# Pairing the score products of the first cross attention on two 64-row tiles of TensorE

## The reference, cut to what matters

```python
def _L0_xattn_ref(query, key_value, mask, Wq, bq, Wk, bk, Wv, bv, Wo, bo):
    E = 128; H = 16; D = E // H            # 16 heads of 8 features
    Q = (query @ Wq.T + bq).reshape(B, Lq, H, D)
    K = (key_value @ Wk.T + bk).reshape(B, Lkv, H, D)
    V = (key_value @ Wv.T + bv).reshape(B, Lkv, H, D)
    scores = jnp.einsum('bqhd,bkhd->bhqk', Q, K) / jnp.sqrt(jnp.float32(D))
    scores = jnp.where(mask[:, None, None, :] == 0, -jnp.inf, scores)
    probs = jax.nn.softmax(scores, axis=-1)
    context = jnp.einsum('bhqk,bkhd->bqhd', probs, V).reshape(B, Lq, E)
    return context @ Wo.T + bo
...
x = x + _L0_xattn_ref(_layernorm(x, axis=-1), ctx_1024, mask_BxS2_ik0, ...)
```

## Time and profile before

| | us |
|---|---|
| Runs of the kernel before | 1927.71, 1927.79, 1922.93 (median 1927.71) |
| Profiled execution | 1924.5, its span 1922.8 |
| TensorE matmul busy in the span | 1362.7 (71%) |
| VectorE busy | 1442.3 (75%) |
| ScalarE busy | 1132.0 (59%) |
| GpSimd busy | 1141.2 (59%) |
| First cross attention, first score to last addition | 205.3 to 437.4 |
| Score products of `x0` on TensorE (L856), busy | 137.7 |
| Masked keys on ScalarE (L994), 128 instructions | 63.0 |

### The profile page before, as it was taken

How to read it: one execution, slowest core, us unless ns; L and a number is a source line. 1 busy time by engine, 2 the same in 40 slices (tenths; PEclk the granted TensorE clock), 3 DMA queues, 4 the chain that set the end, 5 groups by cost and what they waited for, 6 DMA issues and landing times. The chain is left out here.

```text
span 1922.8 us, 23528 instructions
## 1 busy us (share of the span) xinstructions
PE 1362.7 (71%) x6930; PEld 713.1 (37%) x6931; DVE 1442.3 (75%) x2463; ACT 1132.0 (59%) x2507; POOL 1141.2 (59%) x742
## 2 busy tenths in 40 slices
PE   3778899995655566665565656655545899999968
PEld 2555677772311112221112212211102566666522
DVE  3554588885509999999999999999993577666734
ACT  2443888875636556555555665555533777677720
POOL 2001455660029999999999999999980344333400
PEclk8898899997667777877787777777767899999979
DMA  3000000000044324343333333233303000000000
GB/s 104 1 2 2 1 2 1 1 2 1 0 144 188 127 95 154 130 158 154 154 155 118 127 133 151 114 153 154 155 1 88 1 1 1 1 0 1 1 0 22
DMA packets 51978, 134.49 MB, mean 70 GB/s; under 512 B 19076, under 2 KB 28568, under 8 KB 39448
## 3 DMA queue, kind: packets, MB, share of 16 engines
q1 hardware_dynamic: 49112, 130.78, 18.0%
q10 hardware_dynamic: 2496, 2.36, 0.4%
q0 software_dynamic: 256, 0.01, 0.0%
HBM read 114.26 MB, written 18.87 MB: 69 GB/s over the span
## 5 line engine op out<-in xcount | busy, mean ns | idle before, releaser
L1493 POOL TENSOR_TENSOR ma_hs<-ma_dtuR,ma_Bt 128x1024 f32<-128x1024 f32 x256 | 596.9, 2359 | 20.3 <-PE ps L1569 13.5
L1652 ACT ACTIVATE ps<-ma_dtR,ma_A 128x512 f32<-128x512 f32 x512 | 332.6, 682 | 345.2 <-DVE ma_hs L1786 286.7
L809 POOL TENSOR_TENSOR x_pr<-x_pr,x_rec 128x512 f32<-128x512 f32 x256 | 268.0, 1047 | 355.5 <-DVE x_rec L1058 355.5
L1780 DVE TENSOR_TENSOR_SCAN ps<-ps,ma_hs 128x1024 f32<-128x1024 f32 x176 | 401.6, 2282 | 0.0
L1569 PE MATMUL ps<-ma_hs,ma_fold 128*32 128x512 f32 x1024 | 178.9, 834 | 207.7 <-POOL ma_hs L1501 175.7
L1024 ACT ACTIVATE x_pr<-x_sm,x_mx 128x256 f32<-128x256 f32 x512 | 254.6, 500 | 56.1 <-DVE x_mx L1049 55.2
L1786 DVE TENSOR_TENSOR ma_hs<-ps,ma_Ct 128x1024 f32<-128x1024 f32 x176 | 215.4, 1224 | 6.1
L1536 PE MATMUL ps<-ma_hn,ma_w_tap 128*128 128x512 f32 (+3 forms) x256 | 145.4, 722 | 95.7 <-ACT ma_hn L1670 84.0
L1780 DVE TENSOR_TENSOR_SCAN ma_hs<-ps,ma_hs 128x1024 f32<-128x1024 f32 x80 | 182.5, 2281 | 33.4 <-ACT ps L1652 33.4
L1501 POOL TENSOR_TENSOR ma_hs<-ma_hs,ma_Ct 128x1024 f32<-128x1024 f32 x80 | 188.3, 2354 | 22.9 <-DVE ma_hs L1780 22.9
L880 PE MATMUL ps<-ident,x_pr 128*128 128x128 f32 x1024 | 158.8, 279 | 0.8 <-DVE x_pT L955 0.4
(11 more groups left out here) (307 smaller groups left out, 2245.2 us busy)
## 6 DMA issues: line engine op xcount, KB each, us to landing
ma_dtuR<-ma_dtu_d SPq DMA_DIRECT2D x32, 1024.0 KB, 8.0
ma_dtR<-ma_dt_d SPq DMA_DIRECT2D x32, 1024.0 KB, 9.9
ma_Bt<-ma_bc_d SPq DMA_DIRECT2D x16, 1024.0 KB, 4.9
ma_Ct<-ma_bc_d SPq DMA_DIRECT2D x16, 1024.0 KB, 6.8
ma_dtu_d<-ma_dtu SPq DMA_DIRECT2D x32, 256.0 KB, 2.0
ma_dt_d<-ma_dt SPq DMA_DIRECT2D x32, 256.0 KB, 2.3
ma_cwb<-in_L_attn_conv_w_dram SPq DMA_DIRECT2D x4, 512.0 KB
x_m<-in_mask_BxSxS_fk_dram SPq DMA_DIRECT2D x1, 2048.0 KB, 11.2
```

What stands on the lines that cost most here:

```text
L809: pool.tensor_tensor(pr[:, r, :, :], pr[:, r, :, :], rec[:, r, :].unsqueeze(2).broadcast_to([P, 2, L]), ALU.mult).then_inc(pr_done, 1)
L1493: pool.tensor_tensor(hs[:, k % SLOTS, :, :], dtuR[:, unit(f, h), q, :].unsqueeze(1).broadcast_to([P, 2, CH]), rows(Bt, k), ALU.mult).then_ ...
L1652: e = act.activation(c.ps[:, 2 * (k % 2) + a, :], dtR[:, unit(f, h), q, :], ACT.Exp, scale=A[:, (f // QUARTERS) % 2, h, q, no:no + 1])
L1780: dve.tensor_tensor_scan(out, pair(k), slot(k), 0.0, ALU.mult, ALU.add).then_inc(scan_done, 1)
```

## The change

It touches `x0` alone. The recurrent stage of layer 1 (with eleven C products on VectorE) and every other stage are the same in both kernels.

1. `head` maps steps n and n+1 (n even) to two heads a and a+8, whose features lie in rows 0 to 63 and rows 64 to 127.
2. `mine` has two columns per a, for a and a+8; a new reduction on VectorE adds them into `member`. One masked copy of the keys (`keys_of_pair`) then serves both heads, and `km` has 8 entries in place of 16.
3. `score` goes; `x0` uses `score_pair`, in even steps, with the keys from `km`. Four PSUM banks hold scores: 0, 1 and 5, 7 in turn. The wait is that the maximum of head n-3 has been taken.
4. The projections use bank 6 alone, and each waits for the evacuation of the one before it. The three units move to steps 9, 10 and 11.
5. `out_projection` writes bank 6 too. It waits for the last evacuation of the projections, and unit 0 of the next ones waits for `finish`.
6. In `weigh` the four heads of a group take the column tiles in the order 0, 2, 1, 3 in place of 0, 1, 2, 3.

```diff
-    WO = 5 if small else 7
+    WO = 6 if small else 7
+    SCORE_BANKS = ((0, 1), (5, 7)) if small else ((0, 1),)
...
-        return 4 * (n % 4) + n // 4 if small else n
+        return n // 4 + 4 * (n // 2 % 2) + 8 * (n % 2) if small else n
...
         def units(n):

             a = n - FIRST_UNIT
+            if small:
+                return range(a - 1, a) if 1 <= a <= NP else range(0)
             return range(min(NP, a * 3 // 2), min(NP, (a + 1) * 3 // 2)) if a >= 0 else range(0)
...
+        def score_bank(n):
+
+            return SCORE_BANKS[(n // 2) % len(SCORE_BANKS)][n % 2]
+
+        def projection_bank(n):
+
+            return 6 if small else 6 + n % 2
...
                 def project(b, n, first, second):

-                    bank = c.ps[:, 6 + n % 2, :]
-                    if n >= 2:
+                    bank = c.ps[:, projection_bank(n), :]
+                    if small and n >= 1:
+                        pe.wait_ge(evac, b * NP + n)
+                    elif n >= 2:
                         pe.wait_ge(evac, b * NP + n - 1)
                     elif not first:
                         pe.wait_ge(evac, b * NP)
...
-                    if n >= 2 or not first:
+                    if small and (n >= 4 or not first):
+                        pe.wait_ge(max_done, b * NH + n - 2)
+                    elif not small and (n >= 2 or not first):
                         pe.wait_ge(s_free, b * NH + n)
+                    if small:
+                        pe.wait_ge(km_done, b * (NH // 2) + n // 2 + 1)
                     for t in range(2):
                         for r in range(2):
                             row = slice(64 * r, 64 * r + 64)
-                            mm = pe.matmul(c.ps[:, r, t * L:(t + 1) * L], q[row, p, n // 2, t * P:(t + 1) * P],
-                                           k[row, p, n // 2, :], start=True, stop=True)
+                            queries = q[row, p, 0 if small else n // 2, t * P:(t + 1) * P]
+                            keys = km[row, p, n // 2, :] if small else k[row, p, n // 2, :]
+                            mm = pe.matmul(c.ps[:, score_bank(n + r), t * L:(t + 1) * L], queries, keys, start=True, stop=True)
                             if t == 1:
                                 mm.then_inc(scores, 1)
...
-                    if not small and not last:
+                    if not last:
                         pe.wait_ge(evac, b * NP + NP)
...
-                def keys_of_head(b, p, n):
-
-                    h = head(n)
-                    act.activation(km[:, p, h, :], k[:, p, :], ACT.Copy, scale=mine[:, h:h + 1]).then_inc(km_done, 1)
+                def keys_of_pair(b, p, n):
+
+                    a = head(n)
+                    act.activation(km[:, p, n // 2, :], k[:, p, :], ACT.Copy, scale=member[:, a:a + 1]).then_inc(km_done, 1)
...
                 if small:
                     dve.wait_ge(consts, 4)
+                    dve.tensor_reduce(member[:, :], mine[:, :, :], AX.X, ALU.add).then_inc(member_done, 1)
```

More of the change, by code:

```diff
@@ L747, in cross_attention_stage @@
             mr = s.sb("mr", [P, 2, L])
-            km = s.sb("km", [P, 2, NH, L])
-            mine = s.sb("mine", [P, NH])
+            km = s.sb("km", [P, 2, NH // 2, L])
+            mine = s.sb("mine", [P, NH // 2, 2])
+            member = s.sb("member", [P, NH // 2])
         (consts, ctx_in, proj, evac, neg_done, km_done, scores, s_free, shifted, max_done,
-         exp_done, rec_done, pr_done, turned, pT_done, pv, oT_done, out_done, x_done) = (s.sem(n) for n in (
+         exp_done, rec_done, pr_done, turned, pT_done, pv, oT_done, out_done, x_done, member_done) = (s.sem(n) for n in (
             "consts ctx_in proj evac neg_done km_done scores s_free shifted max_done exp_done "
-            "rec_done pr_done turned pT_done pv oT_done out_done x_done").split())
+            "rec_done pr_done turned pT_done pv oT_done out_done x_done member_done").split())
         flat = pr[:, :, :, :].rearrange("p a t k -> p (a t k)")
@@ L794, in _ @@
                     pool.memset(v[:, :, :, :], 0.0).then_inc(consts, 1)
[L795 removed]
+                    pool.memset(mine[:, :, :], 1.0).then_inc(consts, 1)
                     pool.wait_ge(consts, 2)
[L798 to L799 removed]
+                    pool.affine_select(out=mine[:, :, :], in_=mine[:, :, :], compare_op=ALU.is_ge, fill=0.0, base=0,
+                                       pattern=[[-D, NH // 2], [-64, 2]], channel_multiplier=1).then_inc(consts, 1)
                     pool.wait_ge(consts, 3)
[L801 to L802 removed]
+                    pool.affine_select(out=mine[:, :, :], in_=mine[:, :, :], compare_op=ALU.is_ge, fill=0.0, base=D - 1,
+                                       pattern=[[D, NH // 2], [64, 2]], channel_multiplier=-1).then_inc(consts, 1)
                 def body(b, p, fresh, first, last):
@@ L845, in project @@
                     mm.then_inc(proj, 1)
[L847 to L850, removed]
-                    if n >= 2 or not first:
-                        pe.wait_ge(max_done, b * NH + n - 1)
-                    h = head(n)
[L854 to L858, removed]
                 def score_pair(b, p, n, first):
@@ L931, in body @@
                     for n in range(NH):
-                        if small:
-                            score(b, p, n, first)
-                        elif n % 2 == 0:
+                        if n % 2 == 0:
                             score_pair(b, p, n, first)
@@ L999, in _ @@
                     act.wait_ge(evac, NQK)
-                    for n in range(4):
-                        keys_of_head(0, 0, n)
+                    act.wait_ge(member_done, 1)
+                    for n in range(0, 4, 2):
+                        keys_of_pair(0, 0, n)
                 def step(b, p, n, first):
@@ L1012, in body @@
                                 evacuate(b + 1, 1 - p, a, False, first)
-                        if small and n + 4 < NH:
-                            keys_of_head(b, p, n + 4)
-                        elif small and not last:
+                        if small and n % 2 == 0 and n + 4 < NH:
+                            keys_of_pair(b, p, n + 4)
+                        elif small and n % 2 == 0 and not last:
                             if n + 4 == NH:
                                 act.wait_ge(evac, b * NP + NP + NQK)
-                            keys_of_head(b + 1, 1 - p, n + 4 - NH)
+                            keys_of_pair(b + 1, 1 - p, n + 4 - NH)
                         step(b, p, n, first)
@@ L1040, in maximum @@
                     dve.wait_ge(scores, b * NH + n + 1)
-                    bank = c.ps[:, n % 2, :].rearrange("p (t k) -> p t k", t=2)
+                    bank = c.ps[:, score_bank(n), :].rearrange("p (t k) -> p t k", t=2)
                     if n >= 2 or not first:
```

2 lines of the change are left out of this document (removed).

## The result

The change makes the kernel faster by about half of what was forecast. Median 1914.69 us in four runs (1913.99 to 1914.89), against 1925.33 us (1922.93 to 1927.79, four runs) for the kernel before: ratio 0.9944, 95% interval 0.993 to 0.9957, so -10.6 us (-8 to -13.5) where -22.9 was forecast (from 1924.5; between the medians, 1927.7 to 1903, it was -24.7). The profiled execution has 1914.0 us (span 1912.2) against 1924.5 (span 1922.8).

The account below looks back on a forecast made before the run. TensorE was taken to bound `x0`, busy 165.89 of 169.90 us. Six periods falling from 28.3 to 25.2 us save 18.6; with 4.3 + 2.5 - 2.5 at the edges, 22.9: 1924.5 to 1901.6, median 1903, range 1885 to 1919.

Parts of the forecast that it names:

- The loop of 5.67 us through `weigh`: In `x0`, the chain from VectorE's copy through `weigh`, turn and pair to the next group's copy: 5.67 us for four heads.
- the limit of 3: Sign of a wrong forecast in `x0`: the wait before the projection units exceeds 3 us a period.
- the edges: `x0` outside the six middle periods: 4.3 us saved before, 2.5 behind, 2.5 lost at the start.
- the waits add up: Rival in `x0`: extra waits at `weigh` or projections give a 27.0 us period, 1917 us, gain 11; chance 0.18.
- Together 1.8 us a period: Projections of `x0` in one bank: VectorE loses 1.15 and 0.95 us, 0.27 of it already counted; 1.8 us a period.
- the layout from the end of maximum 8: Times through the projections of `x0`: unit 0 at 1.35 us, pair 10 at 2.31, unit 2 at 5.0.
- The 0.58 that the forecast added for `output_bank` and `finish`: In a period of `x0` these two add 0.85 us, of which 0.27 falls into the loop's wait.
- 169.90 / 6 = 28.3: Period of one batch element in `x0` before the change, from seven `output_bank` instructions: 28.3 us.
- The rest of the kernel should only be shifted: Everything from 437 us on, behind `x0`, was to be only shifted in time.
- VectorE's bound: Rival in `x0`: TensorE gets ahead, VectorE sets a 22.5 us period; 1885 us, gain 43, chance 0.16.
- The 0.05 put on the clock: Chance of 0.05 given to the clock; a clock below 0.95 in `x0` would show the forecast wrong.
- The pair without overlap: Rival in `x0`: the two row tiles do not overlap, period 31.1 us, slower by 22; chance 0.01.

Follow-up runs that it names:

- Whole rows: Kernel after with each score product over all 128 rows instead of 64, so a pair cannot share the array: 1934.14 us, ratio 1.0057 to the kernel before.
- two banks: Kernel after with score pairs on two score banks, projections and output bank as before the change: 1951.08 us, ratio 1.0121 to the kernel before.
- finish first, loop written out: Kernel after with `finish` ahead of maximum 8, unit 2 one step later and no hardware loop in `x0`: 1899.28 us, ratio 0.9866.
- Finish first: Kernel after with `finish` ahead of maximum 8 on VectorE and unit 2 one step later, in step 12: 1907.27 us, ratio 0.99.
- The loop written out: Kernel after with the eight batch elements of `x0` written one after another, without the hardware loop: 1909.7 us, ratio 0.9923.
- the shift: Five idle products (2.2 us) ahead of the last output projection of `x1`: kernel after 1915.48 us, ratio 0.995; kernel before 1930.31 us, ratio 1.0029.
- reciprocal and weigh later: Two runs on the kernel after: VectorE's reciprocal one step later, 1916.71 us; `weigh` and `output_bank` one step later, 1935.99 us.
- the filler: Fourteen idle products on TensorE while VectorE picks the experts: kernel after 1914.12 us, ratio 0.9942; kernel before 1925.66 us, ratio 0.9997.

## Why the forecast was right in kind and wrong in size

*Right.* TensorE did bound `x0` before: with 22.8 us less work on it the middle stretch became 12.0 us shorter. The pair took 1.06 us, `weigh` stayed at 1.00 with its new order of tiles (304.73 to 305.73), the clock in the middle of `x0` stayed at 1.00, the copies of masked keys fell to 64, and the loads of TensorE and VectorE became level (143.08 and 139.28 us in six periods). The loop of 5.67 us through `weigh` measured 5.78 to 5.82. The new waits lie where they were foreseen and have about their size (0.78 and 0.60 before the units; the sum of 1.4 stays under the limit of 3). The stretches before and behind the middle are within 0.7 of their forecast. Whole rows show that the overlap is needed for the gain, and two banks show that the spare banks are needed too.

*Where the 12.3 us went.* The sum promised 22.9 and 10.6 came. In the middle stretch 6.6 are missing: 4.0 by the projections (6 x 0.66, the plain period of 25.86 against 25.2), 1.8 by the baseline (6 x 0.3) and 0.9 at the loop's jump. Another 5.8 were lost behind `x0`, where the forecast had no term; the edges nearly cancel. The median lies inside the stated range of 1885 to 1919, but in the part that was given to the rival "the waits add up", and partly because of losses that no rival named.

*The step that failed first: the projections.* "Together 1.8 us a period" measured 8.43 - 5.67 = 2.8. Against the layout from the end of maximum 8 (here 296.75): unit 0 was forecast at 1.35 and came at 1.40; pair 10 at 2.31, came at 2.46; its reader 3.57, came 3.81; unit 2 at 5.0, came 5.26; the reader of pair 12 at 7.2, came 7.68. So the links were each up to 0.1 too short: a unit costs 0.54, not 0.43, and from a pair to its reader are 1.35, not 1.26. (Unit 1 is back at 0.43 with whole rows, 282.10 to 282.53. Unit 2 stands between two whole-array turns and costs 0.54 all the same, so a change of tile shape right beside it is not the whole reason; it stays open.) The larger error was in the adding up. From `weigh` to the end of maximum 8 are 0.45 us, from there to unit 2 5.26, from unit 2 over turn, pair and turn to the next `weigh` 2.72: 8.43. The forecast's own links for the same way are 0.55 (288.84, 289.56 and 290.11 in the earlier trace rows), 5.0 and 2.6, that is 8.2. Its 1.8 counted only what VectorE's two readers lose against undisturbed steps, 5.67 + 1.8 = 7.5, and did not follow TensorE's queue on to the next `weigh`: here TensorE sets the distance, and that `weigh` has no wait. (The 0.58 that the forecast added for `output_bank` and `finish` turned up in the other three groups: 5.78 + 5.82 + 5.97 = 17.6 against 3 x 5.67 = 17.0.)

Seen from VectorE the same miss reads so: its waits, 2.75 us a plain period, were forecast at 2.7 (25.2 - 22.5), but its own time is 139.28 / 6 = 23.2 and not 22.5. The window of the earlier trace rows had it already: 139.33 / 6. A sum over undisturbed steps leaves out that an instruction behind a wait does not overlap the one before. With the same instructions in six periods VectorE is busy 137.92 us with 31 gaps (finish first, loop written out), 139.28 with 44 (the kernel after) and 141.45 with 61 (whole rows), about 0.1 a gap, which is near the overlap of 0.08. Finish first confirms the term of the projections: the waits fell to 1.5, the busy time stayed at 23.0, and the period followed to 24.55.

*The baseline.* "169.90 / 6 = 28.3" is a mean over five plain periods of 28.01 and one of 29.84. So the plain saving was forecast from a period 0.3 too long. What the jump adds to its period did not shrink, it grew from 1.8 to 2.7. VectorE stands about as long at the jump in both kernels, 2.98 us before (at 320.35) and 2.75 after. (The row at 320.35 names a score product, but the one that this maximum needs starts at 315.85 and has ended by 316.9.) Before, however, the maximum behind this one waits 1.05 for its scores in another batch element (291.92), and behind the jump, at 321.71, not at all, so a part of the stall was covered. VectorE's timeline of the kernel before:
```profile
291.92 0.42 DVE L1049 CUSTOM_DVE_ANT_0 x_sm<-ps,x_mr 128x256 f32<-128x256 f32 x1 [1.05 <-PE ps L856]
...
320.35 0.43 DVE L1049 CUSTOM_DVE_ANT_0 x_sm<-ps,x_mr 128x256 f32<-128x256 f32 x1 [2.98 <-PE ps L856]
...
321.71 0.41 DVE L1049 CUSTOM_DVE_ANT_0 x_sm<-ps,x_mr 128x256 f32<-128x256 f32 x1
```
The loop written out takes the stall away, as it should.

*"The rest of the kernel should only be shifted" was wrong.* 4.4 us went into the tail with its expert stage and 1.0 into `x1`. In the tail the difference lies in stretches of lower clock, 0.50 in place of 1.00: the first four records of the expert products take 3.78 us in the kernel after and 3.40 before, but the next four 3.78 against 1.98. The kernel after with the shift had the short tail, which suggests that the low clock hangs on how the code arrives, but one execution does not show it. A pure matter of the moment it is not. The tail is 88.4 to 88.5 in six looped kernels that arrive up to 46 us apart (after, finish first, two banks, reciprocal and weigh later, whole rows), and 84.0 to 87.6 in the seven others. Why the one lot falls on the long stretch stays open.

In `x1` the looped pair kernels take 356.4 to 356.7 us, the kernel before 355.4 (355.3 with the filler), those with `x0` written out 354.0 and 354.2; those with added products in `x1` are left aside. VectorE's timeline of the kernel after shows two idle gaps at its jump that no other engine ends:
```profile
1647.77 0.43 DVE L1105 TENSOR_SCALAR x_neg<-x_m 128x512 f32 x1 [2.74 <-issue]
...
1649.93 0.69 DVE L1049 TENSOR_TENSOR x_sm<-ps,x_m 128x512 f32<-128x512 f32 x1 [1.73 <-issue]
```
The kernel before has the first (2.87) and not the second. The second gap, 1.7 to 1.9 us, is in all eight looped pair kernels and in none of the five others. What decides it is not shown; it was not tried by itself.

*The rivals.* "The waits add up" (period 27.0, 1917) came nearest in time, but only in part by its own way: `weigh` kept no extra 0.5, the projections cost 2.8 where it asked for 3.6, and the period was 25.9; losses outside `x0` did the rest. VectorE's bound needs the round trips out of the way, and even then its 22.5 is not reached: 24.5 is. The 0.05 put on the clock did not come true: in the middle of `x0` it stayed at 1.00, with TensorE busy 91%; a lower clock (0.50) was found in the tail, for which the forecast had no term. The pair without overlap was forecast at 31.1 a period; whole rows measured 28.4, so that rival's price had been too high.

## What to carry to other kernels

When the bound engine is made faster, look for the next period in the longest loop of waits and not in the largest sum of work (here a mean period of 26.3 us, in which TensorE was busy 23.8 and VectorE 23.2): follow the in-order queue from one fixed instruction to its next (`weigh` to `weigh`), with every link taken between its neighbours, and check the sum for each engine against its busy time per period, which also holds the overlap that is lost at waits (about 0.1 us a gap here). Move what starts a round trip (here `finish`) ahead in its engine's queue before anything else, since 1.45 us a period of round trips were worth 7.4 us here, against 10.6 for the whole change. Take a baseline period from plain ones, without the loop's jump (28.01 us here, not 28.3), and expect a few us of difference in the stages that come behind (here 4.4 in the tail and 1.0 in `x1`), which one execution of each kernel can't assign to the change.

## What the runs showed of the hardware

- At the loop's jump back in `x0` VectorE stood idle for 2.75 us in the kernel after (at 313.21), which no other engine ended; with the loop written out this is gone, and the stage is 3.2 us shorter.
- Four products on two 64-row tiles, the scores of two heads, take 1.06 us (kernel after) where four whole-array ones take 1.73 (whole rows). A turn of four transposes between a pair and `weigh` takes 0.59 (304.14 to 304.73, kernel after), between whole-array products 0.44 (291.53 to 291.97, kernel before).
- TensorE's clock stayed at 0.50 for 13 us although its records fill the windows from 1859 to 1871 (kernel after); in the kernel before, the same products had it back at 1.00 within 4 us of 1873.8. Four records of these products take 3.78 us at 0.50 and 1.98 at 1.00. What makes the difference no run here separates.
- The tail of an untouched stage was 4.4 us longer in one kernel than in the other, and in one execution with 2.2 us of added work ahead of it, it was short again.
